# The pass for the maximum of the hidden layer: half of its channels by sums and differences of tokens

## The chip, the cores and the metric

The kernel runs on one core of one Trainium2 chip. The metric is the device time of one execution in microseconds (us), lower is better. TensorE, VectorE, ScalarE and GpSimd each run their own queue of instructions in order, and are tied together by semaphores that the kernel sets by hand.

## The reference

Four blocks stand one after the other on x of 16 batch items, 512 tokens, 256 channels: a cross-attention, a feed-forward with three experts, a second cross-attention whose linear layers quantise their inputs to whole numbers, and a last feed-forward. The change lies in the second cross-attention. Its linear layer, cut to what matters:

```python
def bitnet_linear(x, W, b):
    w_scale = jnp.maximum(jnp.mean(jnp.abs(W)), 1e-05)
    qW = jnp.sign(W) * (jnp.abs(W) > 0.5 * w_scale)
    i_scale = jnp.maximum(jnp.max(jnp.abs(x)), 1e-08) / 127.0
    qx = jnp.clip(jnp.round(x / i_scale), -128.0, 127.0)
    return jnp.einsum('...i,oi->...o', qx, qW) * (w_scale * i_scale) + b
...
concatenated = jnp.concatenate([fused, jnp.broadcast_to(avg_img, (b, s, e))], axis=-1)
h = jax.nn.relu(bitnet_linear(concatenated, W_f1, b_f1))
return bitnet_linear(h, W_f2, b_f2)
```

The scale of a layer's input is one number, the largest absolute value over all items, tokens and channels. So the second layer (W_f2) can't start for any item before the largest value of h (1024 channels) over all 16 items is known.

## The kernel before

The program is a row of blocks, and in each of them every engine has a queue of its own. All engines meet between blocks. The block of the change comes after the attention block, which leaves `ff` (fused activations of all items, channels on partitions: 128 x 16 x 2 x 512, f32), and after a short scale step (`scale_step(A_CAT, ...)`), which turns the largest value into `inv`. It is followed by another scale step (`scale_step(A_H, ...)`), which needs `tmax` from this block, and by the last block, which computes the hidden layer once more, item by item, this time rounds it, and goes on to the output.

The block only finds the maximum. For each of the 16 items n:

- ScalarE scales the item by `inv` and adds a large constant (`qy`, line 4228), then takes the constant off again, which leaves whole numbers of at most 127 in bf16 (`qf[:, n]`, line 4231). The last block uses `qf` again. It runs ahead of the others: no other engine holds it up.
- TensorE multiplies `qf[:, n]` (256 channels in two parts k, 512 tokens) with the ternary weights `wf1` (line 4219). The 1024 hidden channels are eight chunks c of 128. Four PSUM tiles `psum[q]` hold two chunks each, 128 x 1024 f32, so that a group is four matmuls. A group waits until the tile's last content was reduced (`h_red`).
- VectorE reduces each tile over its tokens to two numbers per partition (`hall`, line 4255), one instruction per group, 64 in all.

The bias part of the hidden layer (the mean image embedding) is the same for all tokens of an item. It is computed once at the start (`acc_avg`) and added to `hall` at the end, so the maximum over the tokens may be taken without it. ReLU and the channel's bias follow after the maximum too (lines 4269 to 4274).

The weights of the last block are split into a high and a low part in this block as well: ScalarE copies (line 4238) behind its second item, and VectorE takes the remainders (line 4261) between its second and third item. Items 2 to 15 are a loop on ScalarE and VectorE, items 1 to 15 on TensorE. GpSimd has nothing in this block. No transfer of size runs during it.

Of the kernel before, what the change touches and what calls it, by code (L numbers as in the profile page):

```python
# [18 lines left out]
ALU = mybir.AluOpType  # L19
# [51 lines left out]
def build(nc, a, out):  # L71
# [12 lines left out]
    with ExitStack() as top:  # L84
# [4108 lines left out]
        with ExitStack() as scope:  # L4193
# [6 lines left out]
            round_set, lhi_done = sem("hid_round_set"), sem("hid_weights_hi")  # L4200
            with nc.Block() as block:
                @block.tensor
                def _(pe):
# [7 lines left out]

                    def body(n):
                        for q in range(HC // 2):
                            if q == 0:
                                pe.wait_ge(hq_done, n + 1)
                            after(pe, h_red, 4 * n + q - 3)
                            for c in (2 * q, 2 * q + 1):
                                for k in range(KC):
                                    last = pe.matmul(psum[q][:, (c % 2) * T:(c % 2 + 1) * T], wf1[:, k, c * P:(c + 1) * P],  # L4219
                                                     qf[:, bass.ds(n, 1), k, :].rearrange("p o t -> p (o t)"), start=(k == 0), stop=(k == KC - 1))  # L4220
                            last.then_inc(h_done, 1)
                    first_then_loop(pe, body, B)

                @block.scalar
                def _(s):
                    def body(n):
                        after(s, hq_done, n)
                        s.activation(qy[:, :], ff[:, bass.ds(n, 1), :, :].rearrange("p o k t -> p (o k t)"), ACT.Identity,
                                     bias=pos_round[:, :], scale=inv[:, A_CAT:A_CAT + 1]).then_inc(hy_done, 1)
                        s.wait_ge(hy_done, n + 1)  # L4230
                        s.activation(qf[:, bass.ds(n, 1), :, :].rearrange("p o k t -> p (o k t)"), qy[:, :],
                                     ACT.Identity, bias=neg_round[:, :]).then_inc(hq_done, 1)
                    s.wait_ge(round_set, 2)
                    body(0)
                    body(1)
                    s.wait_ge(l_loaded, 48)
                    for k, name in enumerate(("rT", "kT", "vT")):
                        s.activation(lw[name][0][:, :, :], lstg[:, k, :, :], ACT.Copy, scale=0.5 if name == "vT" else 1.0).then_inc(lhi_done, 1)
                    with s.Fori(2, B) as n:
                        body(n)  # L4240

                @block.vector
                def _(v):
# [7 lines left out]

                    def body(n):
                        for q in range(HC // 2):
                            v.wait_ge(h_done, 4 * n + q + 1)
                            v.tensor_reduce(hall[:, 2 * q:2 * q + 2, bass.ds(n, 1)].rearrange("p c o -> p (c o)"),  # L4255
                                            psum[q][:, :].rearrange("p (c t) -> p c t", c=2), X, ALU.max).then_inc(h_red, 1)
                    body(0)
                    body(1)
                    for k, name in enumerate(("rT", "kT", "vT")):
                        v.wait_ge(lhi_done, k + 1)  # L4260
                        v.scalar_tensor_tensor(out=lw[name][1][:, :, :], in0=lstg[:, k, :, :], scalar=0.5 if name == "vT" else 1.0,
                                               in1=lw[name][0][:, :, :].bitcast(F32), op0=ALU.mult, op1=ALU.subtract)
                    with v.Fori(2, B) as n:
                        body(n)
# [413 lines left out]
```

## Time and profile before

| | |
|---|---|
| median of 3 runs | 1643.27 us (1641.79 to 1643.63) |
| the profiled execution | 1646.63 us, span 1644.6 us |
| instructions | 26214 |
| TensorE busy | 1392.4 us (85%) |
| VectorE busy | 1166.7 us (71%) |
| ScalarE busy | 946.2 us (58%) |
| GpSimd busy | 339.9 us (21%) |
| the block of the change | 1235.5 to 1316.9 us of the span |

The profile is of one execution. The span runs from its first to its last instruction, and the time of an execution is a little longer than its span. Busy time is that of instructions that compute or move data; durations of neighbouring instructions on an engine overlap a little, so the distance between their starts is shorter than the duration of one. The granted clock of TensorE is given as a share of 2.4 GHz, so that 0.5 is 1.2 GHz.

### The profile page before, as it was taken

The numbers are of one execution on the slowest core, as the hardware profiler recorded it, in microseconds if no ns is written. First come the engines' busy times: TensorE is split into PE (matmuls) and PEld (weight loads), VectorE is DVE, ScalarE is ACT, GpSimd is POOL, SyncE is SP. The second block draws the span as 40 slices with busy tenths as digits, with TensorE's granted clock in tenths as the row PEclk, the third lists the DMA queues.
The fourth block names the chain that finished last, engine by engine and source line by source line (L and its number), as shares of the span: only waits on it lengthen the run. The fifth ranks groups of instructions, "written<-read, shape, count | busy, mean of one in ns | idle before, by whom it ended". The sixth has DMA issues, their size and how long they took to land. (4 is left out here: it accounts for less than half of the span.)

```text
span 1644.6 us, 26214 instructions
## 1 busy us (share of the span) xinstructions
PE 1392.4 (85%) x8315; PEld 1107.7 (67%) x8315; DVE 1166.7 (71%) x3017; ACT 946.2 (58%) x1434; POOL 339.9 (21%) x311
## 2 busy tenths in 40 slices
PE   8556679998999999999999878829878869999996
PEld 2335568877888888888888767616543237777775
DVE  5526555677767887777877674418988968898885
ACT  3323334565466655766656445439948048877873
POOL 1101111112111221102211010057400033343330
PEclk9767779999999999999999999958988989999998
DMA  7830133334534655436555566433200011211111
GB/s 201 251 123 18 44 121 112 114 119 166 171 123 135 198 173 157 154 112 198 160 180 168 184 214 201 154 122 103 82 8 1 0 39 39 65 61 54 64 51 38
DMA packets 115446, 192.49 MB, mean 117 GB/s; under 512 B 18256, under 2 KB 84384, under 8 KB 115296
## 3 DMA queue, kind: packets, MB, share of 16 engines
q1 hardware_dynamic: 97408, 146.70, 28.5%
q0 software_dynamic: 13664, 43.28, 7.5%
q10 hardware_dynamic: 4256, 1.07, 0.3%
q8 instruction: 57, 0.93, 0.2%
q14 instruction: 61, 0.50, 0.1%
HBM read 134.10 MB, written 57.98 MB: 117 GB/s over the span
## 5 line engine op out<-in xcount | busy, mean ns | idle before, releaser
L1237 ACT ACTIVATE hr_r<-pair 128x512 f32<-128x512 f32 x136 | 80.7, 593 | 168.9 <-PE pair L161 168.6
L159 PE MATMUL pair<-kv_ring,hr_lo 128*128 128x256 f32 x544 | 161.3, 297 | 7.9 <-DVE hr_lo L3179 6.1
L160 PE MATMUL pair<-kv_ring,hr_hi 128*128 128x256 f32 x544 | 157.7, 290 | 0.0
L161 PE MATMUL pair<-kv_ring,hr_hi 128*128 128x256 f32 x544 | 157.4, 289 | 0.0
L159 PE MATMUL pair<-th_hi,kv_ring 128*128 128x512 f32 x272 | 117.9, 433 | 39.7 <-issue 38.6
L4379 POOL DMA_INDIRECT ff<-x_scratch,slots x64 | 89.3, 1396 | 241.9 <-POOLq L3858 141.3
L1043 POOL DMA_INDIRECT rows_scratch<-row,slot x64 | 64.2, 1004 | 351.1 <-DVE slot L3118 291.2
L4399 ACT ACTIVATE ff<-pair,hbs,s1h 128x512 f32<-128x512 f32 x128 | 95.6, 774 | 54.8 <-PE pair L4469 49.7
L159 PEld LDWEIGHTS pair<-kv_ring,hr_lo 128*128 128x128 f32 x544 | 108.1, 199 | 14.7 <-DVE hr_lo L3179 8.8
L161 PE MATMUL pair<-th_hi,kv_ring 128*128 128x512 f32 x272 | 111.3, 409 | 0.0
L160 PEld LDWEIGHTS pair<-kv_ring,hr_hi 128*128 128x128 f32 x544 | 108.1, 199 | 3.6
L160 PE MATMUL pair<-th_lo,kv_ring 128*128 128x512 f32 x272 | 110.5, 406 | 0.0
L3179 DVE TENSOR_TENSOR hr_lo<-hr_sq,hr_hi 128x512 fp32r<-128x512 f32 x136 | 93.0, 688 | 24.1 <-ACT hr_hi L1244 13.7
L161 PEld LDWEIGHTS pair<-kv_ring,hr_hi 128*128 128x128 f32 x544 | 107.9, 198 | 0.0
L159 PEld LDWEIGHTS pair<-th_hi,kv_ring 128*128 128x128 f32 x272 | 53.1, 195 | 57.2 <-issue 48.5
L1244 ACT ACTIVATE hr_hi<-hr_r 128x512 fp32r<-128x512 f32 x136 | 85.1, 627 | 2.2
L4469 PE MATMUL pair<-qf,wf 128*128 (+1 forms) x256 | 72.1, 394 | 16.5 <-ACT ff L4399 14.2
L3941 POOL DMA_INDIRECT tx<-text_scratch,slots x64 | 69.4, 1084 | 37.9 <-issue 16.9
L4255 DVE TENSOR_REDUCE hall<-pair 128x1024 f32 (+1 forms) x64 | 72.8, 1213 | 3.9 <-PE pair L4219 3.9
L4219 PE MATMUL pair<-qf,wf 128*128 (+1 forms) x256 | 67.5, 399 | 7.8 <-DVE hall L4255 4.0
L3012 DVE TENSOR_TENSOR act_lo<-fm_b,act_hi 128x1024 fp32r<-128x1024 f32 x32 | 39.2, 1224 | 43.2 <-ACT act_hi L1192 24.3
L1934 PE MATMUL pair<-ident,xn 128*128 128x128 f32 x256 | 37.3, 294 | 34.6 <-ACT xn L1134 17.9
(412 smaller groups left out, 4216.9 us busy)
## 6 DMA issues: line engine op xcount, KB each, us to landing
kv_ring<-expert_scratch SPq DMA_DIRECT2D x136, 512.0 KB, 3.8
acc_s<-rows_scratch SPq DMA_DIRECT2D x17, 528.0 KB, 5.4
xn_s<-rows_scratch SPq DMA_DIRECT2D x17, 512.0 KB, 4.1
x_scratch<-acc_s SPq DMA_DIRECT2D x17, 512.0 KB, 5.3
text_scratch<-text SPq DMA_DIRECT2D x17, 512.0 KB, 4.0
x_in<-in_x SPq DMA_DIRECT2D x16, 512.0 KB, 4.8
expert_scratch<-expert_space POOLq DMA_DIRECT2D x2, 4096.0 KB, 18.0
out<-ff SPq DMA_DIRECT2D x16, 512.0 KB, 2.9
```

Source lines behind the costliest of these rows:

```text
L159: pe.matmul(dst, st[1], mv[0], start=start, stop=False, skip_group_check=True)
L160: pe.matmul(dst, st[0], mv[1], start=False, stop=False, skip_group_check=True)
L161: return pe.matmul(dst, st[0], mv[0], start=False, stop=stop, skip_group_check=True)
L1237: s.activation(hr_r[:, c % 2, :], up_ps[:, (c % 2) * T:(c % 2 + 1) * T], ACT.Relu).then_inc(relu_done, 1)
L1244: s.activation(hr_p[0][:, c % RING, :], hr_r[:, c % 2, :], ACT.Square).then_inc(rhi_done, 1)
L3179: v.tensor_tensor(hr_p[1][:, c % RING, :], hr_sq[:, c % 2, :], hr_p[0][:, c % RING, :].bitcast(F32), ALU.subtract).then_inc(rlo_done, 1)
L3941: g.indirect_dma_start(out=tx[l][:, t, :], out_offset=None, in_=text_dram[:, :], in_offset=bass.IndirectOffsetOnAxis(ap=slots[:, n:n + 1], ...
L4219: last = pe.matmul(psum[q][:, (c % 2) * T:(c % 2 + 1) * T], wf1[:, k, c * P:(c + 1) * P], qf[:, bass.ds(n, 1), k, :].rearrange("p o t -> p ...
L4255: v.tensor_reduce(hall[:, 2 * q:2 * q + 2, bass.ds(n, 1)].rearrange("p c o -> p (c o)"), psum[q][:, :].rearrange("p (c t) -> p c t", c=2), ...
L4379: g.indirect_dma_start(out=xt[b % DEPTH][:, t, :], out_offset=None, in_=x3_dram[:, :], in_offset=bass.IndirectOffsetOnAxis(ap=slots[:, n:n ...
L4399: s.activation(hr4[:, c % 4, :], f1_ps[:, (c % 2) * T:(c % 2 + 1) * T], ACT.Relu, bias=hbs[l_ % 2][:, c:c + 1], scale=s1h[:, :]).then_inc( ...
L4469: last = pe.matmul(f1_ps[:, (c % 2) * T:(c % 2 + 1) * T], wf1[:, k, c * P:(c + 1) * P], qf[:, bass.ds(b, 1), k, :].rearrange("p o t -> p ( ...
```

## The change

For the channels of the tiles `psum[2]` and `psum[3]` (half of the 1024), the tokens of an item are paired: t in the first 256, t + 256 in the second. Since the layer is linear, its product with the sum of two tokens is the sum of their products, and the same holds for the difference. The larger of two numbers a and b is half of (a + b) + |a - b|. So:

- GpSimd makes `sd[n % 2]` from `qf[:, n]`: 256 sums and 256 differences for each of the two channel parts, whole numbers of at most 254 in bf16.
- TensorE uses `sd` in place of `qf` for the tiles 2 and 3. The number and size of the matmuls stay. The order of the tiles is now 0, 2, 1, 3 (`PAIRS`).
- ScalarE takes the absolute values of the differences' products out of PSUM (`gap`), two chunks in one instruction.
- VectorE adds them to the sums' products and keeps the largest for each chunk, in one call that also scales by a half: `tensor_tensor_reduce` with a 128x256 output (`larger`) and a 128x1 maximum. It takes two calls for a tile, where one reduction stood before. The tiles 0 and 1 are reduced as before.

All loops over the items are written out. ScalarE no longer runs freely ahead: it rounds item n + 2 between and behind the absolute values of item n, and the weight copies stand ahead of the absolute values of item 1.

```diff
+            sd_done, gap_done = sem("hid_sum_gap"), sem("hid_gap_abs")
+            HT = T // 2
+            sd = [sb(f"hid_sd{l}", [P, KC, 2, HT], BF16) for l in range(2)]
+            gap = [sb(f"hid_gap{l}", [P, 2, HT]) for l in range(2)]
+            larger = [sb(f"hid_larger{l}", [P, HT]) for l in range(4)]
+            PAIRS = (0, 2, 1, 3)
...
                 @block.tensor
...
+                    for n in range(B):
+                        for i, q in enumerate(PAIRS):
+                            if i == 0:
                                 pe.wait_ge(hq_done, n + 1)
-                            after(pe, h_red, 4 * n + q - 3)
+                            if i == 1:
+                                pe.wait_ge(sd_done, n + 1)
+                            if n:
+                                pe.wait_ge(h_red, 4 * (n - 1) + i + 1)
                             for c in (2 * q, 2 * q + 1):
                                 for k in range(KC):
+                                    rhs = qf[:, n, k, :] if q < 2 else sd[n % 2][:, k, :, :].rearrange("p h t -> p (h t)")
                                     last = pe.matmul(psum[q][:, (c % 2) * T:(c % 2 + 1) * T], wf1[:, k, c * P:(c + 1) * P],
-                                                     qf[:, bass.ds(n, 1), k, :].rearrange("p o t -> p (o t)"), start=(k == 0), stop=(k == KC - 1))
+                                                     rhs, start=(k == 0), stop=(k == KC - 1))
                             last.then_inc(h_done, 1)
-                    first_then_loop(pe, body, B)
+
+                @block.gpsimd
+                def _(g):
+                    for n in range(B):
+                        g.wait_ge(hq_done, n + 1)
+                        if n > 1:
+                            g.wait_ge(h_done, 4 * (n - 1))
+                        front, back = qf[:, n, :, 0:HT], qf[:, n, :, HT:T]
+                        g.tensor_tensor(sd[n % 2][:, :, 0, :], front, back, ALU.add)
+                        g.tensor_tensor(sd[n % 2][:, :, 1, :], front, back, ALU.subtract).then_inc(sd_done, 1)
 
                 @block.scalar
                 def _(s):
...
+                    def gaps(n, i):
+                        s.wait_ge(h_done, 4 * n + i + 1)
+                        if n:
+                            s.wait_ge(h_red, 4 * (n - 1) + i + 1)
+                        q = PAIRS[i]
+                        s.activation(gap[q - 2][:, :, :], psum[q][:, :].rearrange("p (c t) -> p c t", c=2)[:, :, HT:T],
+                                     ACT.Abs).then_inc(gap_done, 1)
                     s.wait_ge(round_set, 2)
-                    body(0)
-                    body(1)
-                    s.wait_ge(l_loaded, 48)
-                    for k, name in enumerate(("rT", "kT", "vT")):
-                        s.activation(lw[name][0][:, :, :], lstg[:, k, :, :], ACT.Copy, scale=0.5 if name == "vT" else 1.0).then_inc(lhi_done, 1)
-                    with s.Fori(2, B) as n:
-                        body(n)
+                    for n in range(2):
+                        scaled(n)
+                        rounded(n)
+                    for n in range(B):
+                        if n == 1:
+                            s.wait_ge(l_loaded, 48)
+                            for k, name in enumerate(("rT", "kT", "vT")):
+                                s.activation(lw[name][0][:, :, :], lstg[:, k, :, :], ACT.Copy, scale=0.5 if name == "vT" else 1.0).then_inc(lhi_done, 1)
+                        gaps(n, 1)
+                        if n + 2 < B:
+                            scaled(n + 2)
+                        gaps(n, 3)
+                        if n + 2 < B:
+                            rounded(n + 2)
 
                 @block.vector
                 def _(v):
...
+                    for n in range(B):
+                        if n == 2:
+                            for k, name in enumerate(("rT", "kT", "vT")):
+                                v.wait_ge(lhi_done, k + 1)
+                                v.scalar_tensor_tensor(out=lw[name][1][:, :, :], in0=lstg[:, k, :, :], scalar=0.5 if name == "vT" else 1.0,
+                                                       in1=lw[name][0][:, :, :].bitcast(F32), op0=ALU.mult, op1=ALU.subtract)
+                        for i, q in enumerate(PAIRS):
+                            if q < 2:
+                                v.wait_ge(h_done, 4 * n + i + 1)
+                                v.tensor_reduce(hall[:, 2 * q:2 * q + 2, n], psum[q][:, :].rearrange("p (c t) -> p c t", c=2),
+                                                X, ALU.max).then_inc(h_red, 1)
+                                continue
+                            v.wait_ge(gap_done, 2 * n + q - 1)
+                            if n:
+                                v.wait_ge(h_red, 4 * (n - 1) + i + 1)
+                            for c in range(2):
+                                last = v.tensor_tensor_reduce(larger[2 * (q - 2) + c][:, :], psum[q][:, c * T:c * T + HT], gap[q - 2][:, c, :],
+                                                              0.5, -3.0e38, ALU.add, ALU.max, hall[:, 2 * q + c, n:n + 1])
+                            last.then_inc(h_red, 1)
                     v.wait_ge(h_red, 4 * B)
```

`scaled(n)` and `rounded(n)` are the two ScalarE instructions of lines 4228 and 4231, with their waits.

## Rows read from the trace of the kernel before

**Rows 1.** The page: busy time, share of the span and instructions of each engine.
```profile
PE 1392.4 (85%) x8315; PEld 1107.7 (67%) x8315; DVE 1166.7 (71%) x3017; ACT 946.2 (58%) x1434; POOL 339.9 (21%) x311
```

**Rows 2.** Groups, 1232 to 1318 us: busy us, mean ns of one, idle before and releasers.
```profile
L4255 DVE TENSOR_REDUCE hall<-pair 128x1024 f32 x56 | 63.4, 1212 | 0.0
...
L4219 PEld LDWEIGHTS pair<-qf,wf 128*128 128x128 bf16 x256 | 22.8, 101 | 52.0 <-DVE hall L4255 20.2 <-issue 16.3
L4228 ACT ACTIVATE qy<-ff,pos_round,inv 128x1024 f32 x14 | 17.3, 1239 | 1.6
L4231 ACT ACTIVATE qf<-qy,neg_round 128x1024 f32 x14 | 16.1, 1148 | 1.7
...
L4273 DVE TENSOR_REDUCE tmax<-hmax 128x1 f32<-128x8 f32 x1 | 0.2, 161 | 0.0
```

**Rows 3.** Windows of the stage: busy us (instructions), granted clock; last row, line 4255 alone.
```profile
core 0: us, PE busy (x) PEld busy (x) DVE busy (x) ACT busy (x) POOL busy (x), PEclk, DMA share, GB/s
1235.50:1251.90 16.40, 13.62 (x64) 5.55 (x64) 11.76 (x16) 15.29 (x15) 0.00 (x0) 0.77 0.00 1
1251.90:1315.40 63.50, 54.48 (x208) 17.80 (x208) 63.47 (x57) 24.37 (x21) 0.00 (x0) 0.97 0.00 0
...
1251.90:1315.40 63.50, 63.43 (x56) 0.97 0.00 0
```

**Rows 4.** Waits in the stage: us in total, times, longest us.
```profile
PEld pair L4219 <- DVE hall L4255: 20.2, 38, 0.6
...
DVE hall L4255 <- PE pair L4219: 3.9, 3, 3.1
```

**Rows 5.** Groups of the whole span, by shape, on VectorE, and one on ScalarE.
```profile
L166 DVE BATCH_NORM_STATS2 stat<-x 128x6 f32<-128x256 f32 x128 | 44.7, 410 | 0.0
...
L4131 DVE TENSOR_TENSOR pr<-pair,mx 128x256 f32<-128x256 f32 x32 | 13.6, 424 | 1.1
...
L4149 DVE TENSOR_TENSOR pr<-pr,sm 128x512 f32<-128x512 f32 x16 | 11.1, 692 | 0.6
...
L4029 ACT ACTIVATE prt<-pair 128x512 f32<-128x512 f32 x16 | 9.3, 581 | 7.3 <-PE pair L4097 7.3
```

**Rows 6.** Timeline: start us, duration us, instruction; two small maxima.
```profile
1232.32 0.17 DVE L4180 TENSOR_REDUCE tmax<-curs 128x1 f32<-128x16 f32 x1
1232.41 0.17 DVE L4181 TENSOR_REDUCE tcur<-avg 128x1 f32<-128x32 f32 x1
```

**Rows 7.** Groups of the whole span on GpSimd, by shape.
```profile
L1026 POOL TENSOR_TENSOR rs<-var,neg_half 128x8 f32<-128x8 f32 x16 | 28.5, 1782 | 99.3 <-DVE var L2996 99.3
...
L4371 POOL TENSOR_TENSOR fin_rs<-fin_var,neg_half 128x4 f32<-128x4 f32 x16 | 19.5, 1217 | 79.2 <-DVE fin_var L175 79.2
...
L318 POOL TENSOR_SCALAR_AFFINE_SELECT ident<-ident 128x128 f32<-128x128 f32 x1 | 0.3, 283 | 0.0
...
L4671 POOL MEMSET const-float32-1.0<- 128x1 f32 x1 | 0.1, 100 | 0.0
```

**Rows 8.** Timeline of the stage's start, columns as in rows 6.
```profile
1236.93 1.15 ACT L4231 ACTIVATE qf<-qy,neg_round 128x1024 bf16<-128x1024 f32 x1
...
1240.12 1.23 DVE L4255 TENSOR_REDUCE hall<-pair 128x2 f32<-128x1024 f32 x1 [3.12 <-PE pair L4219]
...
1242.87 5.97 PEld L4219 LDWEIGHTS pair<-qf,wf 128*128 128x128 bf16 x28 [0.28 <-issue]
...
1244.62 1.24 ACT L4228 ACTIVATE qy<-ff,pos_round,inv 128x1024 f32 x1
1245.98 1.15 ACT L4231 ACTIVATE qf<-qy,neg_round 128x1024 f32 x1
...
1250.13 0.68 DVE L4261 SCALAR_TENSOR_TENSOR rT_lo<-lstg,rT_hi 128x512 fp32r<-128x512 f32 x1
...
1251.93 10.27 DVE L4255 TENSOR_REDUCE hall<-pair 128x1024 f32 x9
```

More of the change, by code:

```diff
@@ L4210, in _ @@
                     pe.wait_ge(acc_ready, 1)
-                    def body(n):
-                        for q in range(HC // 2):
-                            if q == 0:
+                    for n in range(B):
+                        for i, q in enumerate(PAIRS):
+                            if i == 0:
                                 pe.wait_ge(hq_done, n + 1)
-                            after(pe, h_red, 4 * n + q - 3)
+                            if i == 1:
+                                pe.wait_ge(sd_done, n + 1)
+                            if n:
+                                pe.wait_ge(h_red, 4 * (n - 1) + i + 1)
@@ L4224, in _, with scaled, rounded @@
                 @block.scalar
                 def _(s):
-                    def body(n):
+                    def scaled(n):
                         after(s, hq_done, n)
-                        s.activation(qy[:, :], ff[:, bass.ds(n, 1), :, :].rearrange("p o k t -> p (o k t)"), ACT.Identity,
+                        s.activation(qy[:, :], ff[:, n, :, :].rearrange("p k t -> p (k t)"), ACT.Identity,
                                      bias=pos_round[:, :], scale=inv[:, A_CAT:A_CAT + 1]).then_inc(hy_done, 1)
+                    def rounded(n):
@@ L4230, in body @@
                         s.wait_ge(hy_done, n + 1)
-                        s.activation(qf[:, bass.ds(n, 1), :, :].rearrange("p o k t -> p (o k t)"), qy[:, :],
+                        s.activation(qf[:, n, :, :].rearrange("p k t -> p (k t)"), qy[:, :],
                                      ACT.Identity, bias=neg_round[:, :]).then_inc(hq_done, 1)
-                    s.wait_ge(round_set, 2)
-                    body(0)
-                    body(1)
-                    s.wait_ge(l_loaded, 48)
-                    for k, name in enumerate(("rT", "kT", "vT")):
-                        s.activation(lw[name][0][:, :, :], lstg[:, k, :, :], ACT.Copy, scale=0.5 if name == "vT" else 1.0).then_inc(lhi_done, 1)
@@ L4250, in _ @@
                     v.tensor_copy(acc_avg[:, :, :].rearrange("p c b -> p (c b)"), psum[3][:, 0:HC * B]).then_inc(acc_ready, 1)
[L4252 to L4264, printed above, removed]
+                    for n in range(B):
[17 more added lines that the diff above has]
+                            last.then_inc(h_red, 1)
```

## The prediction

> **What bounds the kernel now.** I read the page first. TensorE is busy 85% of the span and VectorE 71% [rows 1], but these are averages over stages, so I looked for the stage that the diff touches. The table of groups for its stretch gives the stage's own account: VectorE maxima of 1.21 us each (56 in this row, 8 more listed apart), 256 weight loads with their matmuls, and pairs of ScalarE passes [rows 2]. Split into its start and its steady part, the stage shows VectorE busy for 63.47 of 63.50 us, TensorE for 54.5 of them at a granted clock of 0.97, ScalarE for 24.4, GpSimd for nothing [rows 3]. The waits say the same: TensorE's weight loads stood 20.2 us behind VectorE's maxima, VectorE only 3.9 us behind matmuls, all at the start [rows 4]. So the stage lasts as long as VectorE's queue of maxima, and nothing else of the program runs beside it: the maximum over all items must be known before the next scale, and the last stage waits for that. A microsecond off VectorE here is a microsecond off the end, until another engine takes over.
>
> The price of a maximum in that queue is its pitch, not its duration: 56 of them took 63.43 us [rows 3], 1.133 us each. An item has four, 4.53 us.
>
> **The change part by part.** *VectorE.* Two maxima per item stay: 2.27 us. The other two become four calls that add a 128x256 piece of PSUM to a 128x256 piece of SBUF, scale it, and keep its maximum as a second output. The trace of before has no such call. Below, it can't be cheaper than a plain 128x256 pass with no wait between: 128 of them kept VectorE busy for 44.7 us, 0.349 us each [rows 5]. Above, I let the pass run out in full, 0.424 us for a 128x256 subtraction that reads PSUM, and then charge the second output as a separate small maximum of 0.161 us [rows 2]: 0.585 us. Between them I take 0.349 us plus the distance at which two small independent maxima followed each other, 1232.32 to 1232.41, 0.09 us [rows 6]: **0.44 us**. The row nearest in kind, with no second output, is at the low end, the second output is what is unknown. So the item costs VectorE 2.27 + 4 x 0.44 = **4.03 us** (3.66 at the low bound, 4.61 at the high one).
>
> The Trainium skill has a rule that speaks against the change here: "VectorE: DVE Perf Modes", section "Two Vector instructions with no wait between them", says that an operation which also writes out its accumulator is two instructions, the main one and a read of the accumulator. No row of this trace shows one. By it there would be 128 more instructions on the bounding engine; if each cost a small maximum in full behind a pass at its pitch, 0.349 + 0.161 = 0.51 us, the item would take 4.31 us and the gain would be 1.0 us.
>
> *ScalarE.* Two absolute values per item are added, each over 128x512 of PSUM. The nearest row, a 128x512 pass from PSUM, is 0.581 us [rows 5]. With the two roundings, 1.24 and 1.15 us [rows 2], that is 3.55 us per item in full durations, under 4.03. The three weight copies (128x512, so taken at the same 0.58 us each) now stand ahead of the second item's absolute values.
>
> *GpSimd.* It gets a sum and a difference per item, 128x512 bf16 each. Its trace has no add. A select over 128x128 took 0.283 us, a one-element memset 0.10 [rows 7]: 1.43 ns per element, so 0.83 us for 512 if the second input is free. If each input costs that, 1.56 us. Its small TENSOR_TENSORs (a power) took 1.217 us for 4 elements and 1.782 for 8 [rows 7], so their fixed part is 1.217 - 0.565 = 0.65 us, and with that the upper bound is 0.65 + 512 x 2.86 ns = 2.1 us. I take **1.2 us**, the middle of the first two, since simple operations are nearer in kind than the power. In a sentence by itself: "GPSIMD Engine Reference" of the Trainium skill, section 3.1, has 4497 ns for an add over 2048 fp32, an estimate of 1.12 us for 512; no run here shows it.
>
> Two such calls are hidden if the loop around them closes in time. The sums of item n+2 need its rounding, which stands on ScalarE behind the last absolute value of item n, which needs the last matmul of n. From the second group of matmuls of n to that of n+2: three groups at full rate, 12 x 0.213 (28 weight loads in 5.97 us [rows 8]) = 2.56; absolute value 0.58; rounding 1.15; two GpSimd calls 2X; four semaphores at about 0.1 (the distance by which a full 1.24 us pass and its dependent exceed it: 1244.62 to 1245.98 is 1.36 [rows 8]) 0.4. So two items need 4.7 + 2X, and one 2.35 + X: with X = 1.2 that is 3.55 us, hidden; GpSimd sets the pace from X = 1.68.
>
> *TensorE.* The same 256 matmuls; an item is 16 x 0.213 = 3.41 us at full rate, still under 4.03, and its waits for a freed bank come four groups late as before. A bank's turn (matmuls 0.85, absolute value 0.58, two calls 0.88, three hand-overs 0.3) is 2.6 us, well inside 4.03. Loops written out cost VectorE nothing that the trace shows: it idled for none between maxima.
>
> *The start.* The first maximum is as before, at 1240.12 [rows 8]. The second group now waits for GpSimd: first rounding done at 1238.08, two calls, so at 1240.6 it starts. At half the rate (0.43 us a matmul, the granted clock there being 0.77 on average [rows 3]) it ends at 1242.4, the absolute value at 1243.1, and the queue follows: first-item pairs and maxima to 1246.7, second item's first maximum to 1247.8. Then its absolute value comes behind the second rounding (to 1246.9) and the three copies (1.7), at 1249.2, and the item ends at 1252.1 (pair 0.9, maximum 1.13, pair 0.9). The three weight remainders (1250.13 to 1251.93 before, 1.8 us [rows 8]) end at 1253.9. Before, VectorE began its third item at 1251.93. So the first two items cost **2.0 us** more, though they hold less work.
>
> *The sum.* Fourteen items: 63.4 us before, 14 x 4.03 = 56.4 after. 63.4 - 56.4 - 2.0 = 5.0 us. Nothing behind the stage changes: same scale step, same barrier. In general the gain is 29.6 - 56x us for a call price x (63.4 - 14 x 2.27 - 2.0). The profiled execution took 1646.63 us with a span of 1644.6, 2.0 us around it; the sum makes its span 1639.6. The median of the runs is 3.4 us below the profiled one, and 1643.27 - 5.0 = **1638.3 us**.
>
> **The rivals.** *The calls are cheap* (x = 0.349, the second output hidden in the pass). For it: every plain 128x256 pass shows this pitch. Against it: the extra output must be written somewhere. Item 3.66 us, above TensorE's 3.41 and GpSimd's 3.55; gain 10.1 us, 1633.2.
>
> *The calls are dear* and the change costs time. The mechanism: each call drains before its second output, then that is written, then the next starts, four times an item. At 0.585 us the loss is 3.2 us, 1646.5; if the stream itself ran at half rate, like a 128x512 pass of 0.692 us [rows 5], the item would be 5.04 us and the time 1652.5. It decides from x = 0.53 (no gain), and is seen as slower from 0.59. Against it: the two-input pass that reads PSUM, 0.424 us, runs hardly longer than the one-input statistics, 0.410 us [rows 5].
>
> *GpSimd sets the pace.* For it: no add of this size stands in the trace, and its small TENSOR_TENSORs have the highest fixed price of any engine. Against it: its simple operations are cheap, and it has nothing else to do here. At X = 2.1 an item takes 4.45 us, fourteen 62.3; with 2.0 + 1.8 lost at the start (its two first calls take 0.9 us longer each) the time is 1646.0. No gain from X = 1.93.
>
> *The change hardly moves the time* because calls at 0.48 to 0.58 us eat most of it: 1640.6 to 1646.2.
>
> *TensorE's clock.* At the start it is granted 0.77, and it now pauses there once more. If it stayed at 1.2 GHz, an item would take 16 x 0.43 = 6.9 us, 14 of them 96, and the stage over 30 us more. Against it: it will be busy 3.41 of each 4.03 us, more than the 3.41 of 4.53 that held 0.97 [rows 3].
>
> **How the numbers follow.** The forecast (x from 0.40 to 0.47) has 40 in 100, the cheap calls 15, hardly any change 17, GpSimd's pace 10, dear calls past 0.585 us 15, the clock 3. About 0.2%, 3.3 us, is what a measurement can tell from no change. Faster by more than that: 40 + 15 = 55. Slower: 15 + 3 = 18. Within: 17 + 10 = 27. The range reaches from the low bound of the call's price, 1633, to the high bounds of both unknown prices, 1646.5, with half a microsecond on either side for the error of the start. The likeliest case's own range is 1636 to 1640.
>
> **What would show it.** Right: VectorE busy without a gap from about 1254 to 1310, the distance between first maxima of two items near 4.0 us, absolute values at 0.58 us, GpSimd's calls near 1.2 us and ending before the second group of their item is due, TensorE idle behind VectorE. Wrong: VectorE waiting for absolute values and these for matmuls that wait for GpSimd (its calls over 1.68 us); a distance between the two calls of a pair above 0.53 us; a granted clock near half in the steady part; or a start that costs well over 2 us.

## The result and the profile after

Beside runs of the kernel before (median 1642.61 us), the changed kernel has a median of **1632.18 us** (1630.59 to 1633.95, 4 runs). The ratio is 0.9934, with a 95% interval of 0.9918 to 0.9949: 10.4 us faster, the interval reaching from 8.4 to 13.5. The forecast was 1638.3 us, 5.0 us faster, with a range from 1632.5 to 1647. The direction was right, the size was half of what came, and the time lies 0.3 us below the range. With more runs, on another occasion, the changed kernel was 8.0 us faster by the medians (12 runs beside 23, ratio 0.9951, 0.9926 to 0.9976), so of the 10.4 us some 2 are within the scatter.

The page of the changed kernel has less work on VectorE and more on ScalarE and GpSimd, against [rows 1]:

```profile
PE 1375.0 (84%) x8269; PEld 1102.5 (68%) x8315; DVE 1154.7 (71%) x3113; ACT 961.6 (59%) x1466; POOL 374.4 (23%) x343
```

Groups of the stage, with the columns of [rows 2]. Half of the maxima are left, and the new calls stand beside them:

```profile
L4295 DVE TENSOR_REDUCE hall<-pair 128x2 f32<-128x1024 f32 x32 | 39.0, 1220 | 3.1 <-PE pair L4228 3.1
...
L4302 DVE CUSTOM_DVE_ANT_0 hid_larger<-pair,hid_gap 128x256 f32<-128x256 f32 x64 | 24.3, 416 | 3.2 <-ACT hid_gap L4259 3.2
L4239 POOL TENSOR_TENSOR hid_sd<-qf 128x512 bf16<-128x512 bf16 x16 | 19.2, 1197 | 82.9 <-ACT qf L4251 69.0 <-PE pair L4228 13.9
L4259 ACT ACTIVATE hid_gap<-pair 128x512 f32<-128x512 f32 x32 | 19.1, 596 | 13.1 <-PE pair L4228 12.5
L4240 POOL TENSOR_TENSOR hid_sd<-qf 128x512 bf16<-128x512 bf16 x16 | 18.9, 1182 | 0.0
...
L4302 DVE DVE_READ_ACCUMULATOR2_ANT hall<- 128x1 f32 x64 | 5.2, 82 | 0.0
```

A call lasts 0.416 us, and there are 64 reads of the accumulator besides, at 0.082 us. Absolute values last 0.596 us, GpSimd's calls 1.19. Apart from the reads, these durations are near those of the rows of before; what decides is how close the calls follow each other. The timeline of VectorE in the steady part, start us and duration us:

```profile
1289.69 1.22 DVE L4295 TENSOR_REDUCE hall<-pair 128x2 f32<-128x1024 f32 x1
1290.83 0.41 DVE L4302 CUSTOM_DVE_ANT_0 hid_larger<-pair,hid_gap 128x256 f32<-128x256 f32 x1
1291.17 0.08 DVE L4302 DVE_READ_ACCUMULATOR2_ANT hall<- 128x1 f32 x1
1291.17 0.42 DVE L4302 CUSTOM_DVE_ANT_0 hid_larger<-pair,hid_gap 128x256 f32<-128x256 f32 x1
1291.51 0.08 DVE L4302 DVE_READ_ACCUMULATOR2_ANT hall<- 128x1 f32 x1
1291.51 1.22 DVE L4295 TENSOR_REDUCE hall<-pair 128x2 f32<-128x1024 f32 x1
...
1293.34 1.22 DVE L4295 TENSOR_REDUCE hall<-pair 128x2 f32<-128x1024 f32 x1
```

Two calls with their reads take from 1290.83 to 1291.51, 0.34 us each, the whole half item 1.82 us (1289.69 to 1291.51), and an item 3.65 (to 1293.34). The read of the accumulator starts in the same hundredth as the next call: it lies beside it, not ahead of it.

The windows of the start and of the steady part, with the columns of [rows 3]:

```profile
1229.70:1247.08 17.38, 12.31 (x49) 4.68 (x48) 11.50 (x24) 14.98 (x19) 10.28 (x9) 0.84 0.00 1
1247.08:1298.90 51.82, 47.56 (x203) 19.42 (x208) 51.24 (x141) 39.30 (x48) 27.14 (x24) 0.97 0.00 1
```

VectorE is still busy nearly all the time in the steady part, 51.24 of 51.82 us, and TensorE, now at 47.6, has come close. Fourteen items took 51.8 us in place of 63.5. The start is the timeline below; brackets are idle time before an instruction.

```profile
1233.19 1.23 DVE L4295 TENSOR_REDUCE hall<-pair 128x2 f32<-128x1024 f32 x1 [3.12 <-PE pair L4228]
...
1236.03 0.42 DVE L4302 CUSTOM_DVE_ANT_0 hid_larger<-pair,hid_gap 128x256 f32<-128x256 f32 x1 [1.62 <-ACT hid_gap L4259]
...
1240.84 0.42 DVE L4302 CUSTOM_DVE_ANT_0 hid_larger<-pair,hid_gap 128x256 f32<-128x256 f32 x1 [1.06 <-ACT hid_gap L4259]
...
1243.35 0.69 DVE L4290 SCALAR_TENSOR_TENSOR rT_lo<-lstg,rT_hi 128x512 fp32r<-128x512 f32 x1
...
1243.53 1.52 POOL L4239 TENSOR_TENSOR hid_sd<-qf 128x512 bf16<-128x512 bf16 x1 [2.42 <-ACT qf L4251]
...
1243.96 1.64 DVE L4290 SCALAR_TENSOR_TENSOR kT_lo<-lstg,kT_hi 128x512 fp32r<-128x512 f32 x1
...
1245.01 1.60 POOL L4240 TENSOR_TENSOR hid_sd<-qf 128x512 bf16<-128x512 bf16 x1
...
1245.52 1.64 DVE L4290 SCALAR_TENSOR_TENSOR vT_lo<-lstg,vT_hi 128x512 fp32r<-128x512 f32 x1
...
1247.08 1.21 DVE L4295 TENSOR_REDUCE hall<-pair 128x2 f32<-128x1024 f32 x1
...
1248.44 0.67 PE L4228 MATMUL pair<-qf,wf 128*128 128x512 bf16 x2 [3.73 <-DVE hall L4295]
...
1252.34 0.43 DVE L4302 CUSTOM_DVE_ANT_0 hid_larger<-pair,hid_gap 128x256 f32<-128x256 f32 x1 [0.40 <-ACT hid_gap L4259]
```

VectorE waits 1.62 us for the first absolute value and 1.06 for the second item's, as forecast in kind. Not forecast: two of the three weight remainders take 1.64 us in place of 0.68, while GpSimd's calls beside them take 1.5 to 1.6 in place of 1.15. TensorE, whose next group waits for VectorE, then stands still until 1248.44, and VectorE's wait of 0.40 us at 1252.34 follows from that. The waits of the stage, total, times and longest:

```profile
PEld pair L4228 <- POOL hid_sd L4240: 3.4, 7, 1.3
DVE hid_larger L4302 <- ACT hid_gap L4259: 3.2, 4, 1.6
```

TensorE's weight loads wait for GpSimd a little, seven times. Of VectorE's four waits two lie in the steady part, 0.40 and 0.15 us, both just behind TensorE's pause; from 1255 us on it has none.

The single execution varies more ahead of the stage than the change is worth. VectorE's first maximum started at 1240.12 us before and at 1233.19 after, though nothing ahead of it differs. So I read the stage by its own length, from the start of the first maximum to the addition of `acc_avg` behind the last one. The last column has the timed runs, with the occasion on which they were taken (A to D, before beside them each time):

| kernel | first maximum | stage, us | span behind it, us | span | timed ratio to before (95%) |
|---|---|---|---|---|---|
| before | 1240.12 | 75.28 | 329.2 | 1644.6 |  |
| changed | 1233.19 | 65.72 | 330.8 | 1629.7 | 0.9934 (0.9918 to 0.9949), A |
| loops written out | 1235.23 | 75.10 | 329.1 | 1639.4 | 1.0004 (0.9973 to 1.0034), B |
| plain adds | 1230.73 | 65.49 | 329.0 | 1625.2 | 0.9938 (0.9911 to 0.9964), B |
| one tile | 1234.72 | 71.66 | 329.1 | 1635.5 | 0.9989 (0.9958 to 1.002), B |
| no reads by GpSimd | 1230.32 | 63.01 | 330.7 | 1624.0 | 0.9935 (0.9906 to 0.9965), B |
| third call | 1233.64 | 70.40 | 329.6 | 1633.6 | 0.9995 (0.9981 to 1.001), C |
| late remainders | 1236.72 | 63.55 | 330.7 | 1631.0 | 0.9962 (0.9943 to 0.9981), C |
| rearranged | 1235.97 | 60.44 | 329.4 | 1625.8 | 0.9947 (0.9929 to 0.9965), C |
| three tiles | 1237.19 | 66.30 | 331.2 | 1634.7 | 0.9941 (0.9917 to 0.9965), D |
| changed, again | 1230.04 | 65.74 | 330.8 | 1626.6 | 0.9951 (0.9926 to 0.9976), D |
| rearranged, again | 1240.17 | 60.88 | 329.8 | 1630.8 | 0.9905 (0.9869 to 0.994), D |

By this measure the change is worth 75.28 - 65.72 = **9.56 us** in its stage. Of the 14.9 us between the two profiled spans, 6.9 lie ahead of the stage and are not the change's, 9.6 are the stage's, and 1.6 are given back behind it. That leaves 8.0 us for the stage and what follows, as much as the second comparison of the timed runs. The stage of late remainders holds the three weight remainders, that of rearranged doesn't (they stand behind it). The same kernel repeats its stage within 0.02 us (changed) and 0.44 us (rearranged).

Stage and rest together should give the timed difference, if the part ahead is the same. On the occasions B and D they do, within the intervals; on A the 8.0 us lie just outside (8.4 to 13.5). On C they don't: they have the third call 4.5 us under before, late remainders 10.2 and rearranged 14.6, and the timed ratios say 0.8, 6.2 and 8.7, each outside its interval. B, C and D were taken on three different chips; whether that or something else makes the difference is not known. So a ratio can be off by more than its interval from one occasion to the next, and differences of a few us between kernels are read here from the stage.

### The profile page after: what moved, and what is told of

Read it like the earlier page. It is cut to its first block and busy times, and to the rows that moved or that the text cites. A ratio compares the mean times of both kernels' runs of the same rounds, so it can differ in the third digit from the quotient of the medians.

```text
span 1629.7 us, 26085 instructions
## 1 busy us (share of the span) xinstructions
PE 1375.0 (84%) x8269; PEld 1102.5 (68%) x8315; DVE 1154.7 (71%) x3113; ACT 961.6 (59%) x1466; POOL 374.4 (23%) x343
## 5 line engine op out<-in xcount | busy, mean ns | idle before, releaser
L160 PE MATMUL pair<-kv_ring,hr_hi 128*128 128x256 f32 x544 | 155.5, 286 | 0.0
L161 PE MATMUL pair<-kv_ring,hr_hi 128*128 128x256 f32 x544 | 155.2, 285 | 0.0
L160 PEld LDWEIGHTS pair<-kv_ring,hr_hi 128*128 128x128 f32 x544 | 105.7, 194 | 3.5
L161 PEld LDWEIGHTS pair<-kv_ring,hr_hi 128*128 128x128 f32 x544 | 105.6, 194 | 0.0
L4509 PE MATMUL pair<-qf,wf 128*128 (+1 forms) x228 | 66.6, 399 | 17.9 <-ACT ff L4439 14.0
L1031 POOL TENSOR_TENSOR rs<-var,neg_half 128x4 f32<-128x4 f32 x16 | 19.5, 1218 | 217.5 <-DVE var L175 217.5
L4521 PE MATMUL pair<-wf,hq 128*128 128x256 bf16 x512 | 66.2, 279 | 0.0
```

Source lines behind the costliest of these rows:

```text
L160: pe.matmul(dst, st[0], mv[1], start=False, stop=False, skip_group_check=True)
L161: return pe.matmul(dst, st[0], mv[0], start=False, stop=stop, skip_group_check=True)
L4509: last = pe.matmul(f1_ps[:, (c % 2) * T:(c % 2 + 1) * T], wf1[:, k, c * P:(c + 1) * P], qf[:, bass.ds(b, 1), k, :].rearrange("p o t -> p ( ...
L4521: last = pe.matmul(f2k_ps[:, t * C:(t + 1) * C], hq[l_ % 2][:, c, t * P:(t + 1) * P], wf2[:, c, :], start=False, stop=(c == HC - 1))
```

## The experiments

Theory: the gain is VectorE's shorter item, and the term that I mis-sized is the price of the call. Rivals: the gain comes from the loops written out; GpSimd or ScalarE bounds already; the start is worth more than its sum says. The expectations were on record before each run; the times in them start from the medians of the first comparison, 1642.6 and 1632.2 us. Before itself had 1640.6, 1638.7 and 1642.2 us on the occasions B, C and D, so a ratio says more than a time.

**Loops written out, no pairs**

```diff
-                            if i == 1:
-                                pe.wait_ge(sd_done, n + 1)
...
-                                    rhs = qf[:, n, k, :] if q < 2 else sd[n % 2][:, k, :, :].rearrange("p h t -> p (h t)")
+                                    rhs = qf[:, n, k, :]
...
-                        gaps(n, 1)
...
-                            if q < 2:
+                            if q < 4:
```

> The kernel before with its loops over the items written out and nothing of the pairs: no work for GpSimd, four maxima of 128x1024 per item. Theory (the gain comes from VectorE's shorter item): the time is that of before, 1642.6 us within 1.5, maxima 1.13 us apart, third item to last maximum 63.5 us. Rival (writing the loops out gives a part of the gain, by instructions that arrive without a branch): 1 us or more under before.

Ratio to before 1.0004, interval 0.9973 to 1.0034; medians 1639.23 beside 1640.58 us; stage 75.10 us against 75.28, third item to last maximum 63.4 us. The interval alone would leave room for several us either way; by the stage the loops are worth 0.2 us at most. This run also keeps the changed kernel's order of the tiles, so the order is not the gain either.

**Plain adds in place of the calls**

```diff
+                    v.memset(hall[:, :, :], 0.0)
...
-                                last = v.tensor_tensor_reduce(larger[2 * (q - 2) + c][:, :], psum[q][:, c * T:c * T + HT], gap[q - 2][:, c, :],
-                                                              0.5, -3.0e38, ALU.add, ALU.max, hall[:, 2 * q + c, n:n + 1])
+                                last = v.tensor_tensor(larger[2 * (q - 2) + c][:, :], psum[q][:, c * T:c * T + HT], gap[q - 2][:, c, :], ALU.add)
```

> The changed kernel with the 64 calls that add and keep a maximum replaced by plain adds of the same 128x256 operands. It leaves out the maxima of half of the channels, so the output is wrong. Theory (the second output costs nothing on the queue, the call is a plain 128x256 pass at 0.345 us): the distance between calls stays at 0.345 us and the time at 1632.2 us, within 1. Rival (the reading of the accumulator has a price of 0.03 us or more that a plain pass hasn't): calls at 0.31 us or less, the stage at least 2 us shorter.

VectorE's timeline in the steady part:

```profile
1269.20 1.21 DVE L4296 TENSOR_REDUCE hall<-pair 128x2 f32<-128x1024 f32 x1
1270.33 0.74 DVE L4303 TENSOR_TENSOR hid_larger<-pair,hid_gap 128x256 f32<-128x256 f32 x2
1270.99 1.21 DVE L4296 TENSOR_REDUCE hall<-pair 128x2 f32<-128x1024 f32 x1
```

Two adds take 0.66 us (1270.33 to 1270.99), 0.33 each, where two calls take 0.68. So the second output costs about 0.01 us, not 0 and not the rival's 0.03. The stage is 0.23 us shorter, 65.49, though 64 times 0.01 would be 0.6; VectorE's waits were 0.5 us longer in sum (3.7 us against 3.2). The ratio is 0.9938 (0.9911 to 0.9964). The 0.09 us that I had put on each call is not there.

**One tile by pairs**

```diff
-            PAIRS = (0, 2, 1, 3)
+            PAIRS = (0, 3, 1, 2)
...
-                                    rhs = qf[:, n, k, :] if q < 2 else sd[n % 2][:, k, :, :].rearrange("p h t -> p (h t)")
+                                    rhs = qf[:, n, k, :] if q < 3 else sd[n % 2][:, k, :, :].rearrange("p h t -> p (h t)")
...
-                        gaps(n, 3)
...
-                            if q < 2:
+                            if q < 3:
```

> Only the last of the four tiles goes by pairs. Theory (each tile that goes by pairs saves 1.133 - 2 x 0.345 = 0.44 us per item on VectorE, and nothing else bounds): an item takes 3 x 1.133 + 2 x 0.345 = 4.09 us, fourteen 57.3, so 6.2 us less than before, minus the start's 2: 1638.4 us. Rival (the gain comes mostly from the order or from ScalarE's and GpSimd's new work overlapping differently): item time not 4.09.

VectorE's timeline; the fourth row is three maxima in one:

```profile
1249.08 1.21 DVE L4294 TENSOR_REDUCE hall<-pair 128x2 f32<-128x1024 f32 x1
1250.22 0.41 DVE L4301 CUSTOM_DVE_ANT_0 hid_larger<-pair,hid_gap 128x256 f32<-128x256 f32 x1
...
1250.56 0.41 DVE L4301 CUSTOM_DVE_ANT_0 hid_larger<-pair,hid_gap 128x256 f32<-128x256 f32 x1
...
1250.90 3.47 DVE L4294 TENSOR_REDUCE hall<-pair 128x2 f32<-128x1024 f32 x3
1254.31 0.42 DVE L4301 CUSTOM_DVE_ANT_0 hid_larger<-pair,hid_gap 128x256 f32<-128x256 f32 x1
```

From pair to pair, 1250.22 to 1254.31, an item takes 4.09 us, the number expected. The stage is 71.66 us, 3.6 under before: 6.2 us saved from the third item on, as expected, and 2.5 us lost ahead of it, where I had 2. The remainders were slow here too (1.10, 1.64 and 1.63 us). The timed runs can't tell it from no change: ratio 0.9989, 0.9958 to 1.002.

**GpSimd writes and doesn't read**

```diff
-                        g.tensor_tensor(sd[n % 2][:, :, 0, :], front, back, ALU.add)
-                        g.tensor_tensor(sd[n % 2][:, :, 1, :], front, back, ALU.subtract).then_inc(sd_done, 1)
+                        g.memset(sd[n % 2][:, :, 0, :], 1.0)
+                        g.memset(sd[n % 2][:, :, 1, :], 1.0).then_inc(sd_done, 1)
```

> GpSimd fills the sums and differences with ones by memset instead of reading the tokens, two calls per item as before; the output is wrong. Theory (two of the three weight remainders took 1.64 us in place of 0.69 because they and GpSimd's calls, which took 1.5 to 1.6 in place of 1.15, both read two streams from SBUF at that moment): remainders all at 0.69 us, the third item starts 1.9 us earlier, the clock doesn't fall behind them, the time is 1629.5 us. Rival (ScalarE's or TensorE's new reads slow the remainders): they stay at 1.64 us and the time at 1632.2.

The first call and the three remainders on VectorE:

```profile
1232.65 0.42 DVE L4301 CUSTOM_DVE_ANT_0 hid_larger<-pair,hid_gap 128x256 f32<-128x256 f32 x1 [1.11 <-ACT hid_gap L4258]
...
1240.43 0.69 DVE L4289 SCALAR_TENSOR_TENSOR rT_lo<-lstg,rT_hi 128x512 fp32r<-128x512 f32 x1
1241.03 0.68 DVE L4289 SCALAR_TENSOR_TENSOR kT_lo<-lstg,kT_hi 128x512 fp32r<-128x512 f32 x1
1241.63 0.68 DVE L4289 SCALAR_TENSOR_TENSOR vT_lo<-lstg,vT_hi 128x512 fp32r<-128x512 f32 x1
```

All three are back at 0.68 us, and the stage is 2.7 us shorter, 63.01. Of these, 1.9 are the remainders, 0.5 the first wait (1.11 us in place of 1.62, since a memset takes 0.525 us), and 0.5 the waits behind TensorE's pause (0.40 and 0.15 us), which are gone; about 0.4 come back as small waits in the first two items (0.27 us new, 1.16 in place of 1.06). That makes 2.5 to 2.6 of the 2.7. The clock didn't fall either: TensorE paused for 1.8 us in place of 3.7, and the granted clock of the next 3 us was 1.00 (1242.24 to 1245.24), where the changed kernel had 0.79 and then 0.64 in the 6 us behind its pause (1247.08 to 1253.08). Ratio 0.9935, 0.9906 to 0.9965.

**A third call on GpSimd**

```diff
                         g.tensor_tensor(sd[n % 2][:, :, 0, :], front, back, ALU.add)
+                        if n > 1:
+                            g.wait_ge(sd_done, n - 1)
+                        g.tensor_tensor(spare[n % 2][:, :, :], front, back, ALU.add)
                         g.tensor_tensor(sd[n % 2][:, :, 1, :], front, back, ALU.subtract).then_inc(sd_done, 1)
```

> GpSimd makes a third add of the same size per item, between the sum and the difference, into a spare buffer. Theory (the loop of rounding, GpSimd's calls and three groups of matmuls closes every two items: 4.7 us + GpSimd's calls, now 3 x 1.15): an item takes 4.08 us in place of 3.64, the stage is 6 us longer and the start 1.2: 1639.5 us. Rival (GpSimd's work is hidden as long as it fits in an item, 3.45 under 3.64): the time is 1632 to 1633.5 us.

The timeline, two items apart, with the load that waits between:

```profile
1269.62 0.42 DVE L4306 CUSTOM_DVE_ANT_0 hid_larger<-pair,hid_gap 128x256 f32<-128x256 f32 x1 [0.40 <-ACT hid_gap L4263]
...
1275.86 0.55 PEld L4229 LDWEIGHTS pair<-hid_sd,wf 128*128 128x128 bf16 x4 [1.17 <-POOL hid_sd L4244]
...
1277.57 0.42 DVE L4306 CUSTOM_DVE_ANT_0 hid_larger<-pair,hid_gap 128x256 f32<-128x256 f32 x1 [0.57 <-ACT hid_gap L4263]
```

TensorE waits 1.17 us for GpSimd, and VectorE's waits for absolute values recur every 7.95 us (1269.62 to 1277.57), 3.98 us per item, where the sum over the loop said 4.08 and "hidden while it fits in an item" said 3.65. The stage is 4.7 us longer than the changed kernel's, less than the 7.2 expected. The start costs 2.3 us more, where I had 1.2. The part behind it costs only 2.4 us more, where I had 6, since the waits recur from 1269.62 on and not before: the loop had a lead to use up. One more call of 1.15 us per item, on an engine that is idle half of the time, takes back half of the gain in the stage. By the timed runs it takes back all of it (ratio to before 0.9995, 0.9981 to 1.001), but this is occasion C.

**The remainders behind the last maximum**

```diff
-                        if n == 2:
-                            for k, name in enumerate(("rT", "kT", "vT")):
...
+                    for k, name in enumerate(("rT", "kT", "vT")):
+                        v.wait_ge(lhi_done, k + 1)
...
                     v.wait_ge(h_red, 4 * B)
```

> The changed kernel with the three weight remainders moved behind VectorE's last maximum, where GpSimd has ended. Theory (contention with GpSimd's reads, then TensorE's pause and its fallen clock, cost at the third item): remainders at 0.69 us, TensorE never pauses for 4 us in the stage, 1.9 us from the remainders and up to 1 us from the clock: 1629.5 us. Rival (their place doesn't matter, only their work): 1632.2 us.

The second of the three remainders:

```profile
1299.07 0.68 DVE L4302 SCALAR_TENSOR_TENSOR kT_lo<-lstg,kT_hi 128x512 fp32r<-128x512 f32 x1
```

Remainders of 0.69, 0.68 and 0.68 us, a stage of 63.55 us, 2.2 less than the changed kernel's; ratio to before 0.9962, 0.9943 to 0.9981. The work is the same; only its neighbour on GpSimd is gone. The timed median, 1632.76, doesn't show the 2.2 us; it was taken on another occasion than the changed kernel's, where ratios and stages don't agree.

**Rearranged**

```diff
-            PAIRS = (0, 2, 1, 3)
+            order_of = lambda n: (0, 1, 2, 3) if n == 0 else (0, 2, 1, 3)
+            at = lambda n, q: order_of(n).index(q)
...
-                        if n == 1:
+                        if n == 0:
                             s.wait_ge(l_loaded, 48)
...
                         batch(i, l, 0, bias)
+                        if isinstance(i, int) and i == 0:
+                            for k, name in enumerate(("rT", "kT", "vT")):
+                                v.wait_ge(lhi_done, k + 1)
+                                v.scalar_tensor_tensor(out=lw[name][1][:, :, :], in0=lstg[:, k, :, :], scalar=0.5 if name == "vT" else 1.0,
+                                                       in1=lw[name][0][:, :, :].bitcast(F32), op0=ALU.mult, op1=ALU.subtract)
```

> The changed kernel with three moves: the first item takes its tiles in the order 0, 1, 2, 3, so VectorE has two plain maxima to do while GpSimd makes the first sums; the weight copies stand ahead of the first absolute values, where ScalarE waited 1.8 us; the weight remainders stand at the head of the last block, where VectorE waited 1.6 us for the first ReLU. Theory: of VectorE's waits of 1.62 and 1.06 us in the first two items about 0.8 are left, the 3.7 us of remainders leave the stage and cost 0.3 in the last block, the clock doesn't fall: 1626.5 us. Rival (the last block's start takes back what the stage gives, as its first products then wait for the remainders): 1629 us or more.

The head of the last block on VectorE, the remainders and the first rounding of the hidden layer:

```profile
1301.55 0.68 DVE L4654 SCALAR_TENSOR_TENSOR rT_lo<-lstg,rT_hi 128x512 fp32r<-128x512 f32 x1
...
1302.14 0.68 DVE L4654 SCALAR_TENSOR_TENSOR kT_lo<-lstg,kT_hi 128x512 fp32r<-128x512 f32 x1
...
1302.74 0.68 DVE L4654 SCALAR_TENSOR_TENSOR vT_lo<-lstg,vT_hi 128x512 fp32r<-128x512 f32 x1
...
1303.35 0.42 DVE L4593 TENSOR_SCALAR hq<-ff 128x512 bf16<-128x512 f32 x1
```

The remainders end at 1303.35 and the rounding follows with no wait, where in the changed kernel it had waited 1.58 us for its ReLU. The stage is 60.44 us, 5.3 less than the changed kernel's, and what stands behind it is not longer. Ratio to before 0.9947, 0.9929 to 0.9965; the median of 1628.08 us lies between the 1626.5 of the theory and the rival's 1629, and doesn't decide. The profile does: 329.4 us behind the stage, against 330.8 in the changed kernel and 329.2 before, leave the rival a few tenths at most.

**Three tiles by pairs**

```diff
-            PAIRS = (0, 2, 1, 3)
+            PAIRS = (0, 1, 2, 3)
...
-                                    rhs = qf[:, n, k, :] if q < 2 else sd[n % 2][:, k, :, :].rearrange("p h t -> p (h t)")
+                                    rhs = qf[:, n, k, :] if q < 1 else sd[n % 2][:, k, :, :].rearrange("p h t -> p (h t)")
...
                         gaps(n, 1)
                         if n + 2 < B:
                             scaled(n + 2)
+                        gaps(n, 2)
                         gaps(n, 3)
```

> Three of the four tiles go by pairs, in the order 0, 1, 2, 3, with three absolute values per item on ScalarE. VectorE's item would be 1.133 + 6 x 0.345 = 3.20 us. Theory (ScalarE becomes the bound): by the starts in the changed kernel's trace an absolute value holds ScalarE for 0.49 us, the scaling 1.23 and the rounding 1.1 with its hand-over, so an item takes 3 x 0.49 + 2.33 = 3.8 us, fourteen 53.2 against 50.9 now, the stage 2 us longer than the changed kernel's 65.7. Rival (TensorE, 16 x 0.213 = 3.41 us, or VectorE bounds): an item of at most 3.5 us, the stage 63.7 us or less.

ScalarE's timeline over an item (rounding, absolute value, scaling, two absolute values, rounding):

```profile
1284.79 1.19 ACT L4251 ACTIVATE qf<-qy,neg_round 128x1024 bf16<-128x1024 f32 x1
1285.83 0.64 ACT L4259 ACTIVATE hid_gap<-pair 128x512 f32<-128x512 f32 x1
1286.32 1.27 ACT L4246 ACTIVATE qy<-ff,pos_round,inv 128x1024 f32<-128x1024 f32 x1
1287.45 1.12 ACT L4259 ACTIVATE hid_gap<-pair 128x512 f32<-128x512 f32 x2
1288.40 1.20 ACT L4251 ACTIVATE qf<-qy,neg_round 128x1024 bf16<-128x1024 f32 x1
```

ScalarE has no gap, and the item is 3.61 us (1284.79 to 1288.40), less than my 3.8 (the scaling holds ScalarE for 1.13 us, not 1.23) and hardly less than the 3.65 of two tiles, though VectorE's own work would be 3.2. VectorE now waits 0.34 us per item for an absolute value. The stage is 66.30 us. The ratio, 0.9941 (0.9917 to 0.9965), is that of the change. Between two tiles and three the bound passes from VectorE to ScalarE, and the third tile gains nothing.

**Changed and rearranged, side by side**

> The changed kernel once more, word for word, beside the rearranged one. The stage from first to last maximum takes 65.7 us again, within 0.3, wherever the blocks ahead of it end; the time is 10 us under before, within 3.

> The rearranged kernel once more, beside the changed one. Its stage took 60.4 us against the changed kernel's 65.7, and the rest of the program was as long or 1.4 us shorter. Theory (both differences are real): 1626 to 1628 us where the changed kernel has 1632, a ratio between them of 0.996 to 0.997. Rival (the stage's gain doesn't reach the end): no difference that the timed runs can show.

Changed: median 1634.15 us, ratio to before 0.9951 (0.9926 to 0.9976), stage 65.74. Rearranged: 1626.88, ratio 0.9905 (0.9869 to 0.994), stage 60.88. The stage's gain is seen twice, 5.3 and 4.9 us. The medians are 7.3 us apart. The two intervals against before overlap, but the two kernels set against each other are 7.5 us apart in the mean, with a standard error of 2.6 (12 and 7 runs): the rival is out, the size is open. The rearranged kernel has the shortest stage that was run, and the lowest medians.

## Where the prediction held, and where it failed

**What bounds.** Right before and after: VectorE's queue set the stage, and it still does, busy 51.24 of 51.82 us.

**The price of the call: the step that failed.** "Between them I take 0.349 us plus the distance at which two small independent maxima followed each other". The call costs 0.34, the low bound, and its second output 0.01 of that. An item is 3.65 us in place of my 4.03, so fourteen would be 51.1 us, 5.3 under my 56.4. They took 51.8, as VectorE waited 0.55 us behind TensorE's pause and a little at the end. With the start 0.1 us dearer, 5.0 + 5.3 - 0.7 - 0.1 = 9.5 is the measured 9.56 to a tenth, and the call's price is more than all of what was missing. The row nearest in kind stood at the low end, as I wrote (it was the statistics' row, and not "every plain 128x256 pass"), and there was no row for the surcharge; I took a distance between two instructions that each have a stream of their own to read.

**The rule about two instructions.** By the page "VectorE: DVE Perf Modes" of the Trainium skill, section "Two Vector instructions with no wait between them", such an operation is two instructions. The trace agrees: 64 calls, 64 reads (I had written 128, which is wrong; there are four calls an item). But the price that I derived from it, 0.51 us a call, does not follow: the read overlaps with the next call.

**The start.** My 2.0 us were 2.1: the third item started 13.89 us after the first maximum (1233.19 to 1247.08), before it was 11.81. The agreement is luck. The second item's first call came 7.65 us after the first maximum, where I had 9.08: ScalarE had rounded the third item after 5.6 us, where I had 6.8, and TensorE was at full rate from its third group of matmuls on (0.87 us a group). The rest of that item took 2.51 us for my 2.93, as the calls were cheap there too. Against this, the remainders took 3.73 us for my 1.8, which I had not seen at all. (By its own terms my first item would have ended at 1246.0, not 1246.7; the wait behind it takes that up.)

**GpSimd and the loop.** Its calls took 1.19 us in the mean and 1.15 undisturbed, for my 1.2; that was the middle of a guess from 0.83 to 1.56, so the hit is partly luck. The sum over two items said hidden, at 3.55 us, and it was, with little to spare: the third call shows the loop binding at 3.98 where the sum gave 4.08.

**ScalarE.** 0.596 us for my 0.581. It bounded nothing, as forecast, but one tile more makes it the bound.

**TensorE's clock.** 0.97 in the steady part, as before. But behind the stage I had written "Nothing behind the stage changes". That step failed as well, by 1.6 us. The granted clock in the last block's first 55 us, changed kernel:

```profile
1303.91:1323.91 20.00, 15.73 (x63) 6.35 (x64) 10.85 (x29) 9.34 (x13) 13.11 (x12) 0.76 0.26 79
1323.91:1358.91 35.00, 29.41 (x186) 22.15 (x188) 24.96 (x59) 24.54 (x34) 6.57 (x6) 0.90 0.05 16
```

and in the kernel before, the same stretches counted from the last maximum:

```profile
1320.40:1340.40 20.00, 15.20 (x64) 6.12 (x64) 11.54 (x30) 9.68 (x14) 13.03 (x12) 0.80 0.27 79
1340.40:1375.40 35.00, 29.73 (x198) 22.85 (x199) 25.75 (x65) 25.15 (x34) 6.57 (x6) 0.95 0.06 16
```

In the changed kernel it is 0.76 and 0.90, before it is 0.80 and 0.95, with the same code, and the rest takes 1.6 us longer. The first difference is that TensorE's first 16 matmuls there ran at half rate (7.15 us), before it was the first 12 (5.25 us). Both profiles of the changed kernel have it, and so have no reads, late remainders and three tiles: 0.75 or 0.76 and 0.90 in the same stretches, and 330.7 us or more behind the stage. The others, the third call and the rearranged kernel too, have 0.78 to 0.81 and 0.95, and 329.0 to 329.8 us. What sets it remains open; no experiment was made on it.

**Range and chances.** The cheap call was a rival with 15 in 100, and its 1633.2 us is 1.0 us from the result. Its mechanism held: an item of 3.66 us, measured 3.65. Its 10.1 us hold neither the 0.7 us of waits nor the 1.6 us behind the stage; that the total fits is partly the scatter of the first comparison. A bound of the call's price at the nearest row was right, but I placed the range's end half a microsecond beyond it, while the parts of the program outside of the stage vary by more.

## What to carry to other kernels

Price a new instruction on a full queue by its stream: on VectorE here, a pass over 256 elements cost 0.34 us with a maximum beside it and 0.33 without. Work that is moved to an idle engine closes a loop with the engines that feed it; add up the loop's hand-overs over as many items as it spans, since three calls of 1.15 us, 3.45 in all, against an item of 3.65 already made it the bound. And look at which other queues read SBUF while a two-input pass of VectorE runs: moving three small passes away from them into a wait that was there anyway, with the first item reordered, gave 5 us of the stage, half as much as the change itself.

## What the runs showed of the hardware

A VectorE pass with both inputs in SBUF (the weight remainder, 128x512) took 1.64 us in place of 0.68 while GpSimd added, and GpSimd's adds 1.5 to 1.6 in place of 1.15. The first of the three, which ran already when GpSimd's add began (1243.35 and 1243.53), took its 0.69 us all the same; with one tile by pairs it took 1.10. With GpSimd only writing, by memset, all three took 0.68 or 0.69. The new calls, with one input in PSUM, ran beside the same adds at 0.34 us. "SBUF — State Buffer" of the Trainium skill, section "Who interferes with whom", says that a VectorE instruction with two SBUF inputs contends with a GpSimd instruction that reads SBUF, and not with one that only writes; these traces agree.

GpSimd's add over 128x512 in bf16 took 1.15 us when undisturbed, start to end, and the second of two started 1.1 us behind the first.
